# A four-stage mixture kernel: a new opening and end of the last layer's order, earlier couple loads, and eight dummies in a row

## What is computed

```python
x = x + L0(x, cond)   # expert = argmax(cond[b]); silu(x Wup + bup) * (x Wgate + bgate), times Wdown, + bdown; H = 256
x = x + L1(x, cond)   # x W_base + b_base + 2 * sum over 8 experts of cond[b, e] * (x As_e) Bs_e, rank 16
x = x + L2(x, cond)   # x (sum over 8 of cond[b, g] * weight_g * mask) + bias
x = x + L3(x, cond)   # top-2 of softmax(cond[b]) over 8 experts, each gelu(x Wg) * (x Wu), times Wd; I = 512;
                      # plus the same with one shared set of weights, for all batches
```

## Time and profile before

| | us |
|---|---|
| median of 3 runs | 159.9 |
| lowest, highest | 158.06, 159.93 |
| the profiled execution's own time | 159.88 |
| its span, first to last instruction | 157.9 |
| PE busy in it | 151.5 (96%) |
| POOL busy, DVE busy, ACT busy | 96.4, 113.4, 72.0 |

### The profile page before, as it was taken

One profiled execution on the slowest core, in us unless ns is written; L12 is line 12 of the kernel. 1 busy time (PEld: TensorE's weight loads), 2 busy tenths in 40 slices (PEclk: granted clock), 3 DMA queues, 4 the chain that ended last, 5 costly groups with the idle time before them and its releaser, 6 DMA issues.

```text
span 157.9 us, 3155 instructions
## 1 busy us (share of the span) xinstructions
PE 151.5 (96%) x1076; PEld 137.3 (87%) x1076; DVE 113.4 (72%) x228; ACT 72.0 (46%) x138; POOL 96.4 (61%) x96
## 2 busy tenths in 40 slices
PE   6999999999996899999999999999999999999992
PEld 2458999999984789999999989999999999999881
DVE  2982566666898676588687787786668977768772
ACT  2656444443272355435443545445344543346550
POOL 2000999908889500867996684999493989990000
PEclk9999999999999789999999999999999999999999
DMA  3999888898140558259168739249619119000051
GB/s 79 405 375 360 298 272 269 285 358 359 44 182 28 171 170 226 76 168 268 33 197 281 245 89 318 74 117 324 227 23 304 78 33 341 27 4 0 0 201 69
DMA packets 13336, 29.11 MB, mean 184 GB/s; under 512 B 1272, under 2 KB 7944, under 8 KB 13192
## 3 DMA queue, kind: packets, MB, share of 16 engines
q1 hardware_dynamic: 12896, 27.71, 52.5%
q10 hardware_dynamic: 424, 1.20, 1.9%
HBM read 24.71 MB, written 1.05 MB: 163 GB/s over the span
## 4 chain that ended last, share of the span: by engine, by line
PE 85%; DVE 9%; ACT 2%; issue 1%; DMA 1%; ACTq 0%; DVEq 0%
PE pair L527 23%; PE acc L576 10%; PE pair L464 9%; PE pair L534 9%; PE pair L517 8%; PE acc L561 6%; PE acc L472 5%; PE acc L585 5%; PE pair L443 3%; DVE hid L748 2%; PE pair L453 2%; ACT hid_hi L418 2%; PE pair L496 2%; DVE hid_lo L739 2%; DVE x_hl L713 2%; DVE x L707 1%
## 5 line engine op out<-in xcount | busy, mean ns | idle before, releaser
L739 DVE TENSOR_TENSOR hid_lo<-hid,hid_hi 128x512 fp32r<-128x512 f32 (+1 forms) x41 | 39.2, 957 | 18.2 <-ACT hid_hi L418 17.8
L359 POOL TENSOR_TENSOR duo_lo<-raw_duo,duo_hi 128x512 fp32r<-128x512 f32 x36 | 47.8, 1328 | 2.9
L418 ACT ACTIVATE hid_hi<-hid 128x512 fp32r<-128x512 f32 (+1 forms) x41 | 25.4, 622 | 47.9 <-DVE hid L748 45.9
L356 POOL CAST duo_hi<-raw_duo 128x512 fp32r<-128x512 f32 x36 | 30.7, 853 | 26.4 <-PE acc L576 21.9
L748 DVE TENSOR_TENSOR hid<-pair,act 128x512 f32<-128x512 f32 (+1 forms) x49 | 32.9, 672 | 5.5 <-PE pair L527 3.7
L527 PE MATMUL pair<-x_duo,duo_hi 128*128 128x256 f32 x192 | 36.7, 288 | 0.0
L399 ACT ACTIVATE act<-pair 128x512 f32<-128x512 f32 x48 | 28.3, 589 | 9.7 <-PE pair L527 7.5
L527 PEld LDWEIGHTS pair<-x_duo,duo_hi 128*128 128x128 f32 x192 | 30.7, 194 | 1.0 <-DVE hid L748 0.3
L527 PE MATMUL pair<-x_duo,duo_lo 128*128 128x256 f32 x96 | 27.5, 287 | 0.0
L517 PE MATMUL pair<-x_hl,shared_hi 128*128 128x512 f32 x64 | 20.4, 399 | 0.0
L527 PEld LDWEIGHTS pair<-x_duo,duo_lo 128*128 128x128 f32 x96 | 18.5, 193 | 0.0
(11 more groups left out here) (94 smaller groups left out, 213.5 us busy)
## 6 DMA issues: line engine op xcount, KB each, us to landing
raw_duo<-experts SPq DMA_DIRECT2D x12, 768.0 KB, 5.1
ring<-experts SPq DMA_DIRECT2D x16, 386.5 KB, 4.3
raw_solo<-experts SPq DMA_DIRECT2D x8, 768.0 KB, 5.4
x_duo<-x_hl SPq DMA_DIRECT2D x24, 128.0 KB, 3.8
x<-xT ACTq DMA_DIRECT2D x1, 1024.0 KB, 6.0
raw_solo<-shared SPq DMA_DIRECT2D x1, 768.0 KB, 6.8
out<-lora_raw SPq DMA_DIRECT2D x3, 256.0 KB, 2.9
w_sb<-w SPq DMA_DIRECT2D x1, 512.0 KB, 3.8
```

The lines of the kernel that those rows point to most:

```text
L356: pool.tensor_copy(duo_hi[:, j % HALVES, piece(n)], raw_duo[:, j % RAWS, piece(n)])\
L359: pool.tensor_tensor(duo_lo[:, j % HALVES, piece(n)], raw_duo[:, j % RAWS, piece(n)], duo_hi[:, j % HALVES, piece(n)].bitcast(F32), ALU.su ...
L418: act.activation(hid_hi[:, k % SPLITS, at], hid3[:, u % PAIRS, at], ACT.Copy)\
L739: dve.tensor_tensor(hid_lo[:, k % SPLITS, at], hid3[:, u % PAIRS, at], hid_hi[:, k % SPLITS, at].bitcast(F32), ALU.subtract).then_inc(hid_ ...
```

## The change

```diff
--- before.py
+++ after.py
@@ -73,11 +73,11 @@
 _s = [("S", g, c) for g in range(G) for c in range(C3)]
 _d = [("D", j, h) for j in range(DUOS) for h in range(2)]
 _r = [("R", n, 0) for n in range(SOLOS)]
-ORDER = _s[:4]
+ORDER = _s[:1] + _r[0:1] + _s[1:2] + _r[1:2] + _s[2:4]
 for _n in range(3):
-    _di, _si, _ri = _d[6 * _n:6 * _n + 6], _s[3 * _n + 4:min(3 * _n + 7, 12)], _r[2 * _n:2 * _n + 2]
+    _di, _si, _ri = _d[6 * _n:6 * _n + 6], _s[3 * _n + 4:min(3 * _n + 7, 12)], _r[2 * _n + 2:2 * _n + 4]
     ORDER += _di[0:2] + _si[0:1] + _ri[0:1] + _di[2:4] + _si[1:2] + _di[4:6] + _ri[1:2] + _si[2:3]
-ORDER += _d[18:20] + _r[6:7] + _d[20:22] + _r[7:8] + _d[22:24] + _s[12:16]
+ORDER += _d[18:24] + _s[12:16]
 UNITS = len(ORDER)
 AT = {unit: n for n, unit in enumerate(ORDER)}
 SPLIT_AT = {unit: n for n, unit in enumerate(x for x in ORDER if x[0] != "R")}
@@ -252,10 +252,7 @@
             sp.dma_start(lora_sb[:, :], lora).then_inc(lora_in, 16)
             sp.dma_start(w2_sb[:, :, :], w2).then_inc(w2_in, 16)
 
-            sp.wait_ge(at_done, 1)
-            for b in range(B):
-                if b == SLOTS0:
-                    sp.dma_start(shared_sb, shared).then_inc(shared_in, 16)
+            def load0(b):
                 at = sp.value_load(at_row[0:1, b:b + 1], min_val=0, max_val=E - 1)
                 if b >= SLOTS0:
                     sp.wait_ge(x1_done, b - SLOTS0 + 1)
@@ -286,10 +283,18 @@
                                  x_hl[:, bass.ds(duo_batch[2 * j + n], 1), :, :].rearrange("p b h n -> p (b h) n")
                                  .bitcast(F32)).then_inc(x_duo_in[j % GATHERS], 16)
 
+            sp.wait_ge(at_done, 1)
+            for b in range(SLOTS0):
+                load0(b)
+            sp.dma_start(shared_sb, shared).then_inc(shared_in, 16)
             sp.wait_ge(slots_done, 1)
             duo_expert = values(mybir.EngineType.SP, slot_row[0:1, SLOTS:SLOTS + 2 * DUOS], E)
             load_duo(0)
+            load0(SLOTS0)
+            load0(SLOTS0 + 1)
             load_duo(1)
+            for b in range(SLOTS0 + 2, B):
+                load0(b)
             solo_expert = values(mybir.EngineType.SP, slot_row[0:1, SLOTS + 2 * DUOS:2 * SLOTS], E)
             load_solo(1)
             load_solo(0)
@@ -320,7 +325,6 @@
 
         @block.gpsimd
         def _(pool):
-            pool.memset(zeros[:, :], 0.0).then_inc(zeros_set, 1)
             pool.memset(ones[:, :], 1.0).then_inc(ones_set, 1)
 
             pool.wait_ge(small_in, 16)
@@ -345,9 +349,9 @@
                 .then_inc(shared_done, 1)
 
             for j in range(DUOS):
-                if j == 1:
+                if j == HALVES:
+                    pool.wait_ge(x_lo_done, G)
                     for g in range(G):
-                        pool.wait_ge(lin_read, G + g + 1)
                         pool.tensor_copy(x_sum[:, group(g)], x[:, group(g)]).then_inc(x_copied, 1)
                 pool.wait_ge(duo_in[j % RAWS], 16 * (j // RAWS + 1))
                 if j >= HALVES:
@@ -425,7 +429,7 @@
                     pe.matmul(acc[0][:, :], zeros[:, 0:P], zeros[:, :], start=True, stop=True)
 
             pe.wait_ge(zeros_set, 1)
-            warm(4)
+            warm(8)
 
             pe.wait_ge(ones_set, 1)
             pe.wait_ge(at_diag_done, 1)
@@ -434,7 +438,6 @@
             pe.wait_ge(chosen_done, 1)
             pe.matmul(pair[1][0][0:B, 0:E], cond_sb[:, EARLIER:EARLIER + B], chosen[:, :], start=True, stop=True)
             pe.matmul(pair[1][0][0:B, E:2 * E], ones[:, 0:B], chosen[:, :], start=True, stop=True).then_inc(rank_mm, 1)
-            warm(2)
 
             for q in range(G):
                 pe.wait_ge(bsw_done, q + 1)
@@ -590,9 +593,8 @@
             pe.wait_ge(hid0_done, B * C0)
             pe.wait_ge(shared_done, 1)
             gateup(0)
-            pe.wait_ge(lin_read, G + 2)
+            pe.wait_ge(lin_read, 2 * G)
             gateup(1)
-            pe.wait_ge(lin_read, 2 * G)
             for u in range(UNITS):
                 if u + AHEAD < UNITS:
                     gateup(u + AHEAD)
@@ -600,6 +602,7 @@
 
         @block.vector
         def _(dve):
+            dve.memset(zeros[:, :], 0.0).then_inc(zeros_set, 1)
             dve.wait_ge(cond_in, 16)
             dve.max(top[:, :], cond_sb[:, 0:E]).then_inc(route, 1)
             dve.wait_ge(route, 1)
@@ -619,12 +622,12 @@
             chained(dve.tensor_tensor(onehot[:, :, :], top_at[:, 0:K].unsqueeze(2).to_broadcast([B, K, E]),
                                       cond_sb[:, IOTA:IOTA + E].unsqueeze(1).to_broadcast([B, K, E]), ALU.is_equal))
             dve.tensor_tensor(chosen[:, :], onehot[:, 0, :], onehot[:, 1, :], ALU.add).then_inc(chosen_done, 1)
-            dve.wait_ge(at_mm, 1)
-            dve.tensor_copy(at_row[:, :], acc[1][0:1, 0:B]).then_inc(at_done, 1)
-
             dve.wait_ge(rep_in, 16)
             dve.wait_ge(lora_in, 16)
             for q in range(G):
+                if q == 1:
+                    dve.wait_ge(at_mm, 1)
+                    dve.tensor_copy(at_row[:, :], acc[1][0:1, 0:B]).then_inc(at_done, 1)
                 at = slice(q * GB, (q + 1) * GB)
                 dve.scalar_tensor_tensor(
                     bs_w[:, at, :], lora_sb[:, BS1:BS1 + P].unsqueeze(1).to_broadcast([P, GB, P]), LORA_SCALE,
@@ -751,6 +754,8 @@
             def result(u):
                 unit = ORDER[u]
                 kind, n, part = unit
+                if summed[0] == 0 and additions(unit):
+                    dve.wait_ge(x_copied, G)
                 if unit in END_AT:
                     slots = slots_of(unit)
                     batch = values(mybir.EngineType.DVE, slot_row[0:1, slots[0]:slots[-1] + 1])
@@ -776,8 +781,6 @@
             hidden_low(0)
             low_part(3)
             product(1)
-            hidden_low(1)
-            dve.wait_ge(x_copied, G)
             for u in range(2, UNITS + 2):
                 if 3 <= u <= UNITS and ORDER[u - 1][0] != "R":
                     hidden_low(u - 1)
```

## The result

The changed kernel takes 168.62 us (median of 6 runs, 165.63 to 170.59) against 158.76 us for the kernel before (6 runs): 9.9 us more. The ratio is 1.0517, 95% interval 1.0443 to 1.0592. Every ratio in this document leaves out the executions that lie over 1.5% above the fastest of their kernel, here three of the changed kernel's six (169.25 to 170.59 us), so this one is smaller than the 1.062 of the medians. The profiled execution is one of the longest (170.59 us, span 168.6); a second one is shown among the experiments.

What follows compares the result with a forecast made beforehand. The prediction took PE as the bound, busy 84.61 of 84.65 us at full clock from 60 to 144.65 us. Its sum was 159.88 - 3.05 - 1.9 + 0.4 + 0.2 + 6.7 + 2.7 = 164.93, so 165.0 us, range 161 to 168.5.

Steps and rivals of the forecast that it cites:

- Waits at the end: Couples 10 and 11, no single between: PE stalls 2.2 and 4.5 us for the splits, +6.7 us, at least 5.8.
- The cover argument: At the end, PE work during a split hides it: 2.33 us of 4.5 for couple 10, none for couple 11.
- The allowance that an idle PE would leave DVE idle and POOL unhindered: At the end stalls, splits might fall to their unhindered time, making the waits 5.8 instead of 6.7 us.
- Clock behind the waits: After the two end stalls PE runs at half clock for a while: +2.7 us, bounds 0 and 5.1.
- Opening: Layer 3's opening: 1.71 us idle and 1.7 for the clock go, 0.35 idle comes: -3.05 us, bounds 2.4 and 3.4.
- Start: Kernel start: eight dummies raise the clock some 3.4 us earlier, L443's matmuls cost 3.5 instead of 5.4: -1.9 us, floor 0.
- Ring: Couples 0 and 1 load ahead of ring 10, so PE waits before batch 10: +0.4 us, up to 1.9.
- Single 2: Layer 3's opening: single 2's load stands behind the 12 gathers, R2 waits: +0.2 us, bounds 0 and 1.3.
- x copies: Layer 3's opening: four copies on POOL behind the low parts, 2.4 to 4 us, cost 0, at most 1.
- the one without the clock: Stalls come at the end but the clock stays up: 162.2 us, chance 0.15.
- the one without waits: Couples 10 and 11 aren't held at the end, the gains stand alone: 155.5 us, chance 0.03.
- Rival 3: Ring starves, gates stay shut longer: start +0.4 instead of -1.5, single 2 late by 1.3, clock 4; 169.3 us, chance 0.10.

Runs made afterwards that it cites:

- start_only: Kernel before with the start edits alone (zeros by VectorE, eight dummies in a row, at_row later): 158.61 us, ratio 0.9899.
- three_halves: Changed kernel with three buffers instead of two for the split couples, two tiles placed in dead memory: 159.77 us, ratio 1.0072 to the kernel before.
- best_all: Changed unit order and start edits, old loads, three split buffers, couple 1's split held behind low parts and x copies: 157.45 us, ratio 0.9819 to the kernel before.
- start_again: start_only measured once more, the same start edits on the kernel before: 157.43 us, ratio 0.9879.
- loads_only: Kernel before with SP's new order of loads alone (couple 0 ahead of ring 8, couple 1 ahead of ring 10): 160.02 us, ratio 1.0073.
- stall_dummies: Changed kernel with dummy matmuls on PE ahead of couples 10 (ten) and 11 (twenty-one): 165.36 us, ratio 1.0443 to the kernel before.

## Why the prediction was right, and where it was off

Forecast 165.0 us in a range of 161 to 168.5, slower; measured 168.62 by the median, just above that range, and a ratio of 1.0517, which on the 159.88 us of the sum is 168.1. The direction and the mechanism of the end hold; the size does not. Forecast was 5.1 us more, measured are 9.9 by the medians and 10.7 in the span. The absolute number is off by only 3.6 us because the base was too high by luck: the profiled execution of before was 1.1 us above the median of its later runs. Term by term, against the two profiles:

- **Waits at the end, +6.7: measured 6.9** (2.30 and 4.59). The cover argument holds to 0.2 us. The release of the buffer, the 4.35 us for two pieces (4.36 and 4.32) and the 0.13 ahead of them appear. One reading beside it was wrong without effect: the split of couple 10 was over 3.9 us before that of couple 11 began (140.51 and 144.42), not about 9. The allowance that an idle PE would leave DVE idle and POOL unhindered did not come true: DVE's `hid_lo` took 1.79 us beside couple 11's first subtraction, and the second cast took 1.07, not 0.61. The Trainium skill's rule of an exclusive lock on the shared ports ("SBUF — State Buffer", the section on its two separate sides) holds in this; what I drew from it as a possible saving did not, since the pair's last `hidden_low` was still to run. Timelines of DVE and of POOL at couple 11:

```profile
145.13 1.79 DVE L742 TENSOR_TENSOR hid_lo<-hid,hid_hi 128x512 fp32r<-128x512 f32 x1
```

```profile
146.32 1.07 POOL L360 CAST duo_hi<-raw_duo 128x512 fp32r<-128x512 f32 x1
```

- **Clock behind the waits, +2.7: measured 3.5** in the profiled execution, by removing it (3.41 us at half clock behind the first wait, 4.47 us of work at half clock behind the second). The term was mis-sized by 0.8 here. By the mean clocks half of the ten executions had one such stretch alone, so over all of them it was nearer to the forecast.
- **Opening, -3.05: measured -3.0** between the profiles. But the reason for it is more fragile than the text said. The 1.7 us of the clock were in the profiled execution of before and not in most: of 59 executions beside the experiments 21 have a mean clock of 0.989 like it, at 159.8 to 160.0 us on the average, and 38 a clock of 0.997 to 1.00, at 158.2 to 158.3. That is 1.6 us, in about one execution of three. Against an execution without it the opening gives 1.71 - 0.27 = 1.4 us, and about 2.0 over the mean of all, not 3. Here the step fails that took one profiled execution as typical.
- **Start, -1.9: measured +0.9.** This step failed. The four L446 results (L443 before) started 0.4 us later behind the longer row of dummies, and together took 5.84 us instead of 5.37, since the pace rose later than before and not earlier (ACT's copies, as in the earlier trace rows). The predicted pace exists (the traces of start_only, three_halves and best_all), but not in every execution.

```profile
7.57 0.60 ACT L387 ACTIVATE lora_raw<-pair 128x512 f32<-128x512 f32 x1 [1.69 <-PE pair L446]
9.28 0.60 ACT L387 ACTIVATE lora_raw<-pair 128x512 f32<-128x512 f32 x1 [1.11 <-PE pair L446]
10.54 0.60 ACT L387 ACTIVATE lora_raw<-pair 128x512 f32<-128x512 f32 x1 [0.67 <-PE pair L446]
11.40 0.60 ACT L387 ACTIVATE lora_raw<-pair 128x512 f32<-128x512 f32 x1 [0.26 <-PE pair L446]
```

- **Ring, +0.4: measured +1.9** (the stretch lost 2.1; 0.2 of it is not attributed). Ring 10's load went out at 22.78 instead of 20.53 us, and took 7.87 instead of 3.8. The 4.1 us more in flight are what two couple loads were sized at (4.0 to 4.8). What I left out is SP itself: the load of ring 8 now stands behind the sorted numbers, for which SP waits until 16.94 us, and behind the reading of 24 of them from `slot_row` (1.37 us), which before came after ring 15. The chain of the changed kernel in order of time:

```profile
16.94 1.37 SPq L241
...
22.78 7.87 DMA ring<-experts
...
30.69 1.16 PE pair L467 x8
```

- **Single 2, +0.2: measured 0.** x copies, 0: measured 0 (2.29 us on POOL, over before they are needed).

The sum of the measured terms is -3.0 + 0.9 + 2.1 + 0 + 6.9 + 3.5 = 10.4, against 10.7 in the span. Of the rivals, the one without the clock fell by a look at the windows, the one without waits by the waits. The start and the ring together came out 4.5 us worse than in the sum (+3.0 instead of -1.5). Rival 3 had named this place, at +0.4, and so too small as well. These two terms are most of what the forecast change falls short by, and that is why the time lies at the edge of the range.

## What to carry to other kernels

With a ring of n buffers between a helper engine and a bound engine that runs a fixed program, write down for each refill the bound engine's work between the release and the next use; the wait is the refill's time minus that cover, whatever the helper's average load is. Filler work that needs no refill belongs into the gaps with the least cover, and a third buffer can take its place. Before an edit is credited with a clock gain, look at the granted clock of several executions, and at the spacing of equal matmuls too, since at the start of this kernel the granted clock didn't show what the spacing did. For a moved DMA count what the issuing engine waits for and reads ahead of it.

## What the runs showed of the hardware

- A hole of 1.7 us in PE's stream was followed by 3.4 us at a granted clock of 0.53 in the trace of before, and by full clock in those of start_only, start_again and loads_only, which have the same hole. Of 59 executions of the kernel before 21 have the mean clock (0.989) of the first kind. Holes of 2.1 to 4.6 us were followed by one to three such stretches: by the traces of the changed kernel two and three of them in all, by the mean clocks of its ten executions one to three.
- Dummy matmuls in holes of 2.3 and 4.6 us kept the granted clock at 1.00 behind them (stall_dummies), and PE went on no later than without them.
- Eight dummies of 128x512 in a row from 1.20 to 4.79 us left the first two L443 results behind them at half pace in some executions (copies 1.7 us apart) and at full in others (0.9 us), with the same program. The granted clock reads 1.00 in both.
- A VectorE instruction with two SBUF operands that meets POOL's 1.27 us subtraction took 1.7 to 1.8 us instead of 0.68, and POOL's next cast then 1.07 for 0.61.
